# Three turnovers of a two-layer recurrence, attention and expert network: what stands before and behind the stage barriers

## What is computed

```python
x = x + tanh(g_xattn[0]) * wkv(w, u, layernorm(x), ctx)            # recurrence over time
x = x + tanh(g_ffn[0])   * ffn0(layernorm(x))   # 8 experts, top 2, and a shared FFN
x = x + tanh(g_xattn[1]) * attention(layernorm(x), ctx, ctx)       # 16 heads, causal
x = x + tanh(g_ffn[1])   * ffn1(layernorm(x))   # 64 experts, top 6, capacity 64, shared FFN
```

```python
no = max(o, u + k); A = exp(o - no); E = exp(u + k - no)
y = (A * p + E * v) / (A * q + E)
no2 = max(w + o, k); A2 = exp(w + o - no2); E2 = exp(k - no2)
p, q, o = A2 * p + E2 * v, A2 * q + E2, no2
```

## Time and profile before

| | us |
|---|---|
| median of three runs | 2268.88 (2267.6 to 2269.99) |
| the profiled execution, its own time | 2263.69 |
| its span | 2261.9 |
| PE busy | 1961.1 (87%) |
| DVE busy | 1298.7 (57%) |
| POOL busy | 870.8 (38%) |

### The profile page before, as it was taken

How to read it: one execution, slowest core, us unless ns; L and a number is a source line. 1 busy time by engine, 2 the same in 40 slices (tenths; PEclk the granted TensorE clock), 3 DMA queues, 4 the chain that set the end, 5 groups by cost and what they waited for, 6 DMA issues and landing times. The chain is left out here.

```text
span 2261.9 us, 38805 instructions
## 1 busy us (share of the span) xinstructions
PE 1961.1 (87%) x11898; PEld 1397.6 (62%) x11899; DVE 1298.7 (57%) x3013; ACT 758.5 (34%) x2192; POOL 870.8 (38%) x840
## 2 busy tenths in 40 slices
PE   1988888986999999569999999999999959888886
PEld 1666666664777777347777777777777754433332
DVE  5888888884644444236777777676767632222221
ACT  2333233222422222254555455454554401111110
POOL 5556555543633434152333333333333241212211
PEclk9999999998999999659999999999999989999998
DMA  6432222223333333331111111111111239999996
GB/s 214 162 94 74 87 90 84 84 79 99 104 103 98 100 103 104 125 107 66 67 67 67 66 67 66 67 66 67 66 67 66 100 133 410 409 400 406 406 400 208
DMA packets 113561, 319.48 MB, mean 141 GB/s; under 512 B 31298, under 2 KB 39490, under 8 KB 105220
## 3 DMA queue, kind: packets, MB, share of 16 engines
q1 hardware_dynamic: 86388, 264.83, 31.2%
q0 software_dynamic: 26880, 52.68, 8.1%
q10 hardware_dynamic: 144, 0.03, 0.0%
HBM read 257.33 MB, written 62.33 MB: 141 GB/s over the span
## 5 line engine op out<-in xcount | busy, mean ns | idle before, releaser
L1567 ACT ACTIVATE attn_pr<-attn_score_ps,attn_nmax 128x128 f32<-128x128 f32 x496 | 201.9, 419 | 201.4 <-DVE attn_nmax L1720 201.4
L1678 POOL DMA_INDIRECT list<-attn_pair,attn_pos x192 | 192.0, 1000 | 72.3 <-issue 61.1
L328 PE MATMUL attn_ffn_ps<-attn_xnT_high,attn_wgu_high 128*128 128x256 f32 x704 | 208.9, 297 | 9.1 <-DVE attn_hT_low L1812 8.2
L328 PE MATMUL attn_ffn_ps<-attn_xnT_low,attn_wgu_high 128*128 128x256 f32 x704 | 200.4, 285 | 0.0
L328 PE MATMUL attn_ffn_ps<-attn_xnT_high,attn_wgu_low 128*128 128x256 f32 x704 | 200.3, 284 | 0.0
L300 POOL TENSOR_SCALAR attn_norm_var_eps<-attn_norm_mean_var 128x2 f32<-128x2 f32 x32 | 7.9, 248 | 469.6 <-DVE attn_norm_mean_var L294 469.5
L527 PE MATMUL wkv_ffn_ps<-wkv_xnT,wkv_wg 128*128 128x256 f32 x512 | 146.7, 437 | 25.3 <-DVE wkv_x L842 24.2
L1965 POOL DMA_INDIRECT out<-routed_ym,routed_place x32 | 50.2, 1569 | 300.5 <-DMA out<-routed_ym,routed_place 275.1
L1720 DVE TENSOR_REDUCE attn_nmax<-attn_score_ps 128x2 f32<-128x256 f32 x248 | 126.2, 551 | 62.2 <-PE attn_score_ps L1409 61.2
L328 PEld LDWEIGHTS attn_ffn_ps<-attn_xnT_high,attn_wgu_high 128*128 128x128 f32 x704 | 136.0, 193 | 19.7 <-DVE attn_hT_low L1812 13.1
L1011 POOL DMA_INDIRECT y<-routed_ys,first_ffn_pair x72 | 73.5, 1021 | 183.6 <-DVE routed_ys L1161 179.4
(11 more groups left out here) (286 smaller groups left out, 4792.9 us busy)
## 6 DMA issues: line engine op xcount, KB each, us to landing
second_ffn_room<-in_w_gu SPq DMA_DIRECT2D x16, 2816.0 KB, 37.9
routed_wgu<-in_w_gu SPq DMA_DIRECT2D x16, 2816.0 KB, 38.2
second_ffn_room<-in_w_down SPq DMA_DIRECT2D x16, 1536.0 KB, 31.3
routed_wdn<-in_w_down SPq DMA_DIRECT2D x16, 1536.0 KB, 31.2
wkv_x<-in_x SPq DMA_DIRECT2D x32, 512.0 KB, 4.0
second_ffn_room<-y SPq DMA_DIRECT2D x32, 512.0 KB, 5.4
wkv_vT<-in_ctxT SPq DMA_DIRECT2D x16, 512.0 KB, 4.2
xn<-wkv_xn SPq DMA_DIRECT2D x16, 512.0 KB, 2.8
```

The costliest lines, as they stand in the source:

```text
L328: ins = nc.tensor.matmul(out, a[i], b[j], start=start and n == 0, stop=stop and n == 2)
L1567: nc.scalar.activation(pr[u % 2][:, a, j:2 * j + 1, :].rearrange("p k t -> p (k t)"), score_ps[:, a, KEYS[j]], ACT.Exp, bias=nmax[u % 2][: ...
L1678: nc.gpsimd.indirect_dma_start(io["list1"], bass.IndirectOffsetOnAxis(ap=pos[b.s][:, j, k:k + 1], axis=0), pair[b.s][:, j, k, :], None, bo ...
```

## The change

- **Start.** The setup stage is gone as a stage. Its pieces are methods of a class `Setup` and run inside the recurrence's block. SP loads x and vT of batch 0 first, then the four small arrays, the weights, batch 1, and then makes the five stores. POOL makes the constants first and waits for the five stores (`begin.stored`) before its turns. DVE does the norm of batch 0 and the drift and decay, then setup's part.
- **Recurrence to experts 0.** SP loads the first two pieces of the list (READY0 = 2) instead of three; it waits for the xn stores, the scatters and the weights before the table's steps and not after; it stores the last x2 as its last step without waiting for it to land. ACT waits for x2's stores before the fifth expert's weights (KEPT = 4). POOL's three gathers move into the next block, the third behind the first low part, and the third piece of the list is loaded there.
- **Attention to experts 1.** For the last batch PE's order is logits, logits_back, two groups, ranks, four groups. DVE makes one `hidden` before `slots`. SP doesn't wait for the last x3 store; POOL waits for it before the first add. POOL's waits for xn stores go, and the wait for the list of pairs and three gathers move behind the barrier.

The diff, cut to its core (Setup's methods hold setup's statements, word for word):

```diff
-WAYS0, SLOTS0, AHEAD0 = 8, 4, 3
+WAYS0, SLOTS0, AHEAD0, READY0 = 8, 4, 3, 2
...
+class Setup:
...
+    def tensor(self, nc, pe):
+        pe.wait_ge(self.loaded, 64)
+        pe.wait_ge(self.made, 2)
+        nc.tensor.matmul(self.gates_ps[:, 0:4], self.ones_row[:], self.gates_in[:], start=True, stop=True).then_inc(self.spread, 1)
+        pe.wait_ge(self.made, self.MADE)
...
+        dve.wait_ge(dve_s, 9)
...
                 load(FIRST)
+                begin.loads(sp, io)
                 sp.wait_ge(wr_zero_s, 1)
                 for t, name in ((wr[:, :, 0:E0], "gate_w0"), (wr[:, :, E0:E0 + 1], "se_gate"),
                                 (wg[:], "sh_gate"), (wu[:], "sh_up"), (wd[:], "sh_down")):
                     sp.dma_start(t, io[name].rearrange("(k p) n -> p k n", p=P),
                                  allow_slow_non_contiguous=name == "se_gate").then_inc(weights_in, 16)
                 load(FIRST.after())
+                begin.stores(sp, io)
                 turns(sp, B, turn)
                 sp.wait_ge(y_done, B)
                 for e in range(E0):
                     sp.dma_start(c.early.wdn[:, :, e, :], io["w_down0"][e].rearrange("(k p) n -> p k n", p=P)).then_inc(c.weights0_in, 16)
                 store_xn(LAST)
                 store_x2(LAST.before())
-                sp.wait_ge(table, TABLE_STEPS0)
-                for s in range(2):
-                    sp.wait_ge(scat[s], 16 * TJ * K0 * (B // 2))
-                for i in range(AHEAD0):
-                    c.early.load_pair(sp, io, i, i)
-                store_x2(LAST)
                 sp.wait_ge(c.weights0_in, 16 * 2 * E0)
                 for s in range(2):
                     sp.wait_ge(xn_out[s], 16 * (B // 2))
-                    sp.wait_ge(x2_out[s], 16 * (B // 2))
+                    sp.wait_ge(scat[s], 16 * TJ * K0 * (B // 2))
+                sp.wait_ge(table, TABLE_STEPS0)
+                for i in range(READY0):
+                    c.early.load_pair(sp, io, i, i)
+                store_x2(LAST)
...
+                begin.tensor(nc, pe)
                 pre(FIRST)
...
                 norm_pre(FIRST)
@@ -705,21 +712,19 @@
                         values(b.after())
 
                 nc.gpsimd.memset(wr[:], 0.0).then_inc(wr_zero_s, 1)
+                begin.pool(nc, pool)
+                pool.wait_ge(begin.made, begin.MADE)
                 nc.gpsimd.iota(time_no[:], [[1, T]], base=0, channel_multiplier=0,
                                allow_small_or_imprecise_dtypes=True).then_inc(time_s, 1)
                 norm1.pool(nc, pool, FIRST)
                 pool.wait_ge(init_s, 2 * KC + 1)
                 undrift(FIRST)
                 values(FIRST)
+                pool.wait_ge(begin.stored, begin.STORED)
                 turns(pool, B, turn)
                 norm2.pool(nc, pool, LAST)
                 scatter(LAST.before())
                 scatter(LAST)
-                for s in range(2):
-                    pool.wait_ge(xn_out[s], 16 * (B // 2))
-                for i in range(AHEAD0):
-                    pool.wait_ge(c.early.pair_in[i], 16)
-                    c.early.gather(nc, io, i)
 
             @block.vector
...
+                dve.wait_ge(x_in[0], 16)
+                norm1.dve(nc, dve, FIRST, x[0])
+                dve.wait_ge(begin.loaded, 64)
                 for ins in (v.tensor_scalar(w_up[:], c.w[:], 0.0, None, ALU.max), v.tensor_scalar(w_down[:], c.w[:], 0.0, None, ALU.min)):
                     ins.then_inc(time_s, 1)
                 dve.wait_ge(time_s, 3)
                 v.tensor_tensor(u_up[:], c.u[:], w_up[:], ALU.add).then_inc(time_s, 1)
                 v.engine_nop().then_inc(freed, 2)
-                v.tensor_reduce(fold[:], c.ident[:].rearrange("p (k e) -> p e k", k=KC), AX.X, ALU.add).then_inc(fold_s, 1)
-                dve.wait_ge(x_in[0], 16)
-                norm1.dve(nc, dve, FIRST, x[0])
                 for k in range(KC):
                     v.tensor_scalar(drift[:, k, :], time_no[:], w_up[:, k:k + 1], None, ALU.mult).then_inc(init_s, 1)
                 dve.wait_ge(w_exp_s, 1)
@@ -920,6 +925,8 @@
                 dve.wait_ge(init_s, 2 * KC)
                 v.memset(decay[:, :, 0:1], 0.0).then_inc(init_s, 1)
                 dve.wait_ge(init_s, 2 * KC + 1)
+                begin.vector(nc, dve)
+                v.tensor_reduce(fold[:], c.ident[:].rearrange("p (k e) -> p e k", k=KC), AX.X, ALU.add).then_inc(fold_s, 1)
                 turns(dve, B, turn)
...
+        KEPT = 4
...
-                    if isinstance(t.i, int) and t.i < AHEAD0:
+                    if isinstance(t.i, int) and t.i < READY0:
...
+                gather(first(TILES0, WAYS0))
+                gather(first(TILES0, WAYS0).after())
                 gate_up_low(0)
+                gather(first(TILES0, WAYS0).after().after())
                 turns(pool, TILES0, turn, WAYS0)
...
                 def gate_up_high(e):
+                    if e == KEPT:
+                        for s in range(2):
+                            act.wait_ge(c.x2_out[s], 16 * (B // 2))
...
-                    sp.wait_ge(x3_out[s], 16 * (B // 2))
...
                 ffn_inputs(LAST)
-                for u in range(UNITS):
-                    behind(LAST, u)
+                logits(LAST)
+                logits_back(LAST)
+                for n in range(2):
+                    gate_up(LAST, n)
+                ranks(LAST)
+                for n in range(2, M1):
+                    gate_up(LAST, n)
...
-                for s in range(2):
-                    pool.wait_ge(xn_out[s], 16 * (B // 2))
-                pool.wait_ge(c.late.pairs_in, 16)
-                for i in range(AHEAD1):
-                    c.late.gather(nc, io, i)
...
                 choose(LAST)
-                for n in range(2):
-                    hidden(LAST, n)
+                hidden(LAST, 0)
                 slots(LAST)
-                for n in range(2, M1):
+                for n in range(1, M1):
                     hidden(LAST, n)
...
-                    if not q.first:
+                    if q.first:
+                        for s in range(2):
+                            pool.wait_ge(c.late.x3_out[s], 16 * (B // 2))
+                            alone(pool)
+                    else:
                         pool.wait_ge(added[q.before().s % SLOTS1], 16 * uses(q.before()))
                         alone(pool)
...
+                pool.wait_ge(c.late.pairs_in, 16)
+                for i in range(AHEAD1):
+                    c.late.gather(nc, io, i)
                 unrolled(pool, PAIRS1, turn, WAYS1)
                 add(last(PAIRS1, WAYS1).before())
                 add(last(PAIRS1, WAYS1))
...
-            for phase in (setup, wkv_phase, routed0_phase):
+            for phase in (wkv_phase, routed0_phase):
```

170 lines of the change are left out of this document (83 added, 87 removed).

## The result

The changed kernel takes 2248.23 us (median of 5 runs, 2246.89 to 2256.8) where the kernel before, in 5 runs beside it, takes 2268.88. The ratio over all runs is 0.992, with an interval of 0.9902 to 0.9937, which is 14 to 22 us less; the two medians alone differ by 20.65 (0.991). The forecast was 2246.9. The profiled execution took 2247.82 us, its span is 2246.1 and PE's mean granted clock 0.95; its span is 15.8 us shorter than the profiled one of before, of 22.0 that the sum gave.

The account below looks back on a forecast made before the run. PE was taken as the busy engine over the whole span, with gains read around each barrier. 5.3 + 8.0 + 8.7 = 22.0 us off the profiled 2263.69 gives 2241.7; the median, 5.2 above, 2246.9; range 2240 to 2256.

Parts of the forecast that it names:

- Start, 5.3 forecast: Recurrence's start: x of batch 1 lands 7.5 us earlier, less 2.2 for waiting on stores, net 5.3.
- the 2.2 for the stores' wait: Start: POOL's wait for five stores, in 4 to 5 us after batch 1's x, makes its norm some 2.2 later.
- First turnover, 8.0 forecast: Recurrence to experts 0: SP opens the stage 9.6 us earlier, but gathers come behind it; first product 8.0 earlier.
- issued at 539.6: Experts 0: first gather's issue time in us, right behind the stage's opening at 539.45; landing 3.6 later.
- Second turnover, 14.65 forecast: Attention to experts 1: POOL's drain ends at 1847.3, so the stage opens 14.65 us earlier, at 1848.2.
- DVE's last residual ends at 1846.75: End of attention: the last residual's end in us, following from hiddens that end 4.5 earlier.
- The 4.5 of the hiddens: Last batch of attention: hiddens end 4.5 us earlier, from 2.4 and 3.3 less 1.2 for PE's groups.
- Payback, 6.0 forecast: Last stage: gathers landing late beside the weights cost 6.0 us, 2.5 of later stream and 3.4 of leftover adds.
- A (backlog): Rival, end of attention: POOL's drain works off 1.99 us per indirect DMA; opening only 6.4 earlier, 2253.3 us; chance 0.20.
- B (gathers slip in): Rival, experts 1: first gathers slip between the weights, so the payback of 6.0 goes; 2240.9 us; chance 0.12.
- C (the start gives nothing): Rival, start: the stores' landing paces the first turn; 16.7 us gained in all, 2252.2; chance 0.12.
- D (slower): Rival, experts 1: first gathers take 37.9 to 40.3 us like weight loads, stalling the stream; 2274 us; chance 0.03.

Follow-up runs that it names:

- e1: Changed kernel with POOL's wait for the five setup stores moved from its first turn to its first scatter; PE's first transposes at 34.78 us, 2.4 earlier than the mean.
- e12: e1 with the three first gathers of experts 1 put back ahead of attention's barrier; median 2250.73 us, ratio 0.9921 to the kernel before.
- e2: Changed kernel with the first two gathers of experts 0 put back ahead of the recurrence's barrier; table to first product 17.51 us instead of 11.59.
- e6: Changed kernel with experts 1's gate and up weight loads in four pieces and down weights in two; last stage 407.9 us against 404.6.
- e9: e1 with x and vT of the second batch loaded ahead of the 3 MB of shared weights; PE's first transposes at 36.05 us, in e1 34.78.
- e7: Changed kernel with SP awaiting experts 1's first two gathers before issuing its first weights; attention's last norm to span's end 448.8 us against 449.7.
- e5: Changed kernel with each gate and up weight load of experts 1 issued as two, down weights as before; last stage 403.9 us against 404.6.

## Why the prediction was right, point by point

The steps of the sum gave 5.3 + 7.1 + 12.7 - 5.6 = 19.5 us of the forecast 22.0, and 3.6 more went in between, in a place where the sum had nothing; that makes the 15.8 of the spans. That the medians differ by 20.65, so near to 22.0, is in part luck: the profiled execution of before lay 5.2 us under its median and that of the changed kernel 0.4.

- **Start, 5.3 forecast, 5.3 measured** (5.2 on the mean of eight). The 7.5 of the x load held, and so did the 2.2 for the stores' wait (2.25 by e1 and e12). How the 2.2 came about did not: the wait ended at 23.90, 5.6 behind the start of the statistics and not 4 to 5, so the norm began 3.7 later relative to them and not 2.2. But the norm's four steps, which POOL before made beside DVE's scans in 5.6 us, took 4.0. The two misses cancel, which is luck.
- **First turnover, 8.0 forecast, 7.1 measured.** Who opens the stage (SP), that POOL's drain is over before, the landing of the gather (3.5) and the rest (2.8) held. The step that failed is "issued at 539.6", 0.15 behind the opening: POOL's first instruction starts 0.9 behind, at 535.38 where ACT starts at 534.57.
- **Second turnover, 14.65 forecast, 12.7 measured.** The slots (7.2 earlier forecast, 7.1 measured) and the drain (7.2 and 6.9 behind the last indirect DMA) held. The step that failed is "DVE's last residual ends at 1846.75", that is 4.5 earlier: it was 2.7. The 4.5 of the hiddens nearly held, for the last products of PE, which wait for them, begin 4.2 earlier, counted from the last norm (1828.40, before 1841.36). The rest was lost in these products. PE made the first half of them in 6.2 us instead of 4.7, at a granted clock of 0.77 to 0.80 (in 1826 to 1834 us); it had been busy for 1.6 of the first 4 us. Before, in 1838 to 1842, it had been busy for 1.6 of 4 as well and was granted 1.00, so why the clock fell stays open. It doesn't always cost this much: of the eleven executions with the new order the last residual starts 41.1 to 41.4 behind the norm in six and 42.4 to 42.7 in five, the changed kernel's both among them (before, 45.4). In e2, e6 and e9 the weights started 43.6 to 43.8 behind the last norm, 14.1 earlier than before: there the forecast's figure nearly held.
- **Payback, 6.0 forecast, 5.6 measured.** The number is near by luck, for both of its terms failed. Right was that the first gathers land late (10.1), so that PE's first work came 10.7 us later and the first add 10.4. But of the 2.5 by which the stream was to end later only 0.4 came (370.9 behind the first weights, before 370.5), and the adds left over behind the stream, my 3.4, cost 0.5: the last add starts 2.0 us behind the last copy, before 1.5. In their place PE's last result came 4.8 later, and this is the chain I hadn't seen: POOL issues a gather only after the add before it in its program, so late adds made late gathers, and PE waited for them 34.6 us. In e7, where the first gathers aren't late, PE's waits for gathers in midstream and the 4.8 are both gone. In e5 the waits are gone too, but there the slower stream takes their place.
- **What no step had:** between the first product of experts 0 and attention's last norm 3.6 us of the gain went, 3.3 of them in attention. Past the first turn, from one batch's norm to the next it takes 52.5 us at best in every kernel, and up to 56.3 (before), 56.1 (changed) or 58.0 (e7) otherwise. The first two rows are windows of 5 us in such a turn of e7 (57.7 us), the others the same place of that turn in the kernel before (53.9):

```profile
1317.00:1322.00 5.00, 3.41 (x16) 2.84 (x18) 3.87 (x7) 3.10 (x11) 4.36 (x4) 0.71 0.66 241
...
1322.00:1327.00 5.00, 5.00 (x28) 2.79 (x27) 1.20 (x3) 2.10 (x10) 4.27 (x3) 0.61 0.25 90
```

```profile
1328.40:1333.40 5.00, 4.44 (x29) 2.78 (x28) 4.05 (x8) 3.16 (x11) 3.82 (x3) 1.00 0.72 273
...
1333.40:1338.40 5.00, 5.00 (x43) 4.00 (x41) 1.18 (x3) 1.98 (x9) 4.52 (x4) 1.00 0.30 108
```

The columns are as above; the clock is the first figure behind the brackets, 0.71 and 0.61 there (1.00 is 2.4 GHz and 0.50 is 1.2), 1.00 here. PE had been busy 4.9 of the 5 us ahead of the first. These dips fall differently in each execution. Attention was shortest, 875.6 us, in the profiled execution of before, whose time was 5.2 under its median. Whether an earlier start of attention brings more dips isn't settled, since 875.6 us is one execution. The mean granted clock of the whole span doesn't show it (0.949 before, 0.950 changed).
- **Rivals.** A (backlog) is excluded by the drains. B (gathers slip in) didn't happen: the first two landed in 10.1 and 11.3. The Trainium skill's rule, that an engine goes round its queues packet by packet ("DMA: Bandwidth & Descriptors", Queues, rings and completion order), was read in the prediction as a gather that slips through at once, and the 10.1 us speak against that reading. They don't speak against the rule. The same place gives a packet 9 to 17 descriptors; if a row is a descriptor, then all 8 rows of a load on one engine fit in one packet, and at 405 GB/s over 16 engines 8 rows of 22.5 KB are 7.1 us, an estimate. A gather landed in 3.6 in idle queues, and 3.6 + 7.1 = 10.7 is near the 10.1. That smaller pieces of weights let a gather through sooner (e5, e6) agrees as to the kind. C (the start gives nothing) and D (slower) are out with 5.3 us and with landings of 10.1.

## What to carry to other kernels

Look at what a barrier waits for besides the engines' last instructions. Here POOL's queue drained 5.5 to 7 us behind its last indirect DMA, though that had landed in 2 to 4, so gathers issued just ahead of a barrier are dear. A transfer whose first reader is far on can be waited for there. Work moved behind a barrier is worth what it opens less what it delays: where the next stage fills the DMA engines at once, the two were equal within what the runs can tell; where it doesn't (experts 0), the move was worth 5.9 us. An order that brings the last indirect DMAs forward was worth 6 to 8 us. And read a cost from the event just before it: the stores' wait was 2.25 us in every execution, counted from DVE's statistics, while the table behind it moved by 2.3 us on its own.
